# A fused decoder layer on one core: TensorE's semaphore waits moved ahead of the last two matmuls of the group in front

## The reference

```python
x = layernorm(x + self_attn(x))              # 128 sequences of 128 tokens, D = 256, 16 heads of 64, causal
x = layernorm(x + cross_attn(x, ctx, mask))  # 16 heads of 16, keys masked, biases
x = layernorm(x + ffn(x))                    # two groups of 32 experts, hidden 128, top 2 of each, SwiGLU
```

## Time and profile before

| | |
|---|---|
| median of 3 runs | 4513.68 us (4513.43 to 4518.73) |
| the profiled execution | 4515.24 us, span 4513.5 us |
| TensorE busy over the span | 4395.4 us (97%), 38848 matmuls |
| VectorE, ScalarE, GpSimd busy | 3689.1 (82%), 3288.8 (73%), 2752.3 us (61%) |
| TensorE busy, 300 to 3,200 us | 2897.93 us |
| granted TensorE clock | 0.99 over the span |

### The profile page before, as it was taken

How to read it: one execution, slowest core, us unless ns; L and a number is a source line. 1 busy time by engine, 2 the same in 40 slices (tenths; PEclk the granted TensorE clock), 3 DMA queues, 4 the chain that set the end, 5 groups by cost and what they waited for, 6 DMA issues and landing times. The chain is left out here.

```text
span 4513.5 us, 129797 instructions
## 1 busy us (share of the span) xinstructions
PE 4395.4 (97%) x38848; PEld 3808.0 (84%) x38848; DVE 3689.1 (82%) x18057; ACT 3288.8 (73%) x12741; POOL 2752.3 (61%) x3747
## 2 busy tenths in 40 slices
PE   7999999999999999999999999999995899999998
PEld 6888888888888888888888888888884778878876
DVE  4788888888888888888888888888886466658888
ACT  5888888888888888888888888888884444444443
POOL 3466666666666566666665666666656455557777
PEclk9999999999999999999999999999997999999999
DMA  5121221111221211112211111112115599988998
GB/s 169 47 71 65 68 68 62 65 66 64 68 67 66 67 65 65 66 64 67 69 66 66 67 65 65 65 64 71 65 60 166 177 356 343 315 284 285 309 307 287
DMA packets 477421, 552.08 MB, mean 122 GB/s; under 512 B 55632, under 2 KB 408144, under 8 KB 476240
## 3 DMA queue, kind: packets, MB, share of 16 engines
q1 hardware_dynamic: 350800, 296.21, 20.5%
q0 software_dynamic: 52224, 146.87, 8.6%
q10 hardware_dynamic: 73728, 100.70, 7.3%
HBM read 266.21 MB, written 277.35 MB: 120 GB/s over the span
## 5 line engine op out<-in xcount | busy, mean ns | idle before, releaser
L898 ACT ACTIVATE prob<-prob,negmax 128x128 f32<-128x128 f32 x2048 | 796.5, 391 | 298.0 <-DVE negmax L1032 298.0
L898 ACT ACTIVATE xprob<-xprob,xnegmax 128x128 f32<-128x128 f32 x2048 | 797.8, 396 | 4.3 <-DVE xnegmax L1032 4.3
L1364 POOL DMA_INDIRECT y_d<-y,to x576 | 563.9, 979 | 352.2 <-DVE y L1506 325.8
L1032 DVE CUSTOM_DVE_ANT_0 prob<-bank,causal 128x128 f32<-128x128 f32 x2048 | 453.1, 285 | 303.2 <-PE bank L787 277.8
L634 POOL DMA_INDIRECT xs_d<-xrow,place x512 | 561.8, 1097 | 134.0 <-issue 133.0
L1417 PE MATMUL bank<-moe,xgT 128*128 x2304 | 595.4, 381 | 0.9 <-issue 0.6
L597 POOL TENSOR_TENSOR rs<-spread_v,minus_half 128x1 f32<-128x1 f32 x256 | 146.8, 573 | 644.1 <-DVE spread_v L1106 643.9
L1080 DVE TENSOR_TENSOR xprob<-xprob,xinv 128x512 f32<-128x512 f32 x512 | 482.9, 943 | 17.5
L580 POOL CAST yTh<-yT 128x512 fp32r<-128x512 f32 x256 | 206.0, 805 | 441.1 <-ACT yT L934 441.1
L685 PE MATMUL bank<-xT0h,wqkv 128*128 128x256 f32 x2048 | 437.4, 298 | 20.4 <-DVE wqkv L434 11.3
L1032 DVE CUSTOM_DVE_ANT_0 xprob<-bank,xmask 128x128 f32<-128x128 f32 x2048 | 451.6, 286 | 0.3 <-PE bank L787 0.3
(11 more groups left out here) (174 smaller groups left out, 13327.6 us busy)
## 6 DMA issues: line engine op xcount, KB each, us to landing
xg<-xs_d SPq DMA_DIRECT2D x576, 129.0 KB
xs_d<-blank SPq DMA_DIRECT2D x248, 272.0 KB
rows<-y_d ACTq DMA_DIRECT2D x256, 256.0 KB
xT_s<-xT SPq DMA_DIRECT2D x128, 128.0 KB, 2.5
cT<-cT SPq DMA_DIRECT2D x128, 128.0 KB, 2.1
x_s<-x SPq DMA_DIRECT2D x128, 128.0 KB
x_d<-x SPq DMA_DIRECT2D x128, 128.0 KB, 1.9
sums<-x_d ACTq DMA_DIRECT2D x128, 128.0 KB
```

What stands on the lines that cost most here:

```text
L898: last = nc.scalar.activation(dst[:, h, :], dst[:, h, :], ACT.Exp, bias=src_bias[:, h:h + 1], scale=-1.0, accum_out=acc[:, h:h + 1])
L1032: last = nc.vector.tensor_tensor_reduce(dst[:, h, :], heads(h), bias[:, :], -1.0, float("inf"), ALU.add, ALU.min, least[:, h:h + 1])
L1364: nc.gpsimd.indirect_dma_start(y_d[:, :], bass.IndirectOffsetOnAxis(ap=to[:, m % NTO:m % NTO + 1].bitcast(U32), axis=0), y_s[q][:, :], Non ...
```

## The change

Each group is cut in two functions: one with its waits (`..._needs`) and one with its matmuls, which takes as argument `ahead` a function that makes the waits of the group behind it. It is called ahead of the last two matmuls (of `x1t`, `x2t`, `o2`, `xv` and `route`, which have only two, ahead of all). Where a group isn't live in a step, `ahead` is called in its place. Two waits stay at the head of their group: that of `xq` (behind `v1`), and that of `rank` (behind `xk`). `score` of the next step is waited for inside `cross_mix`. The waits are the same semaphores and values, the matmuls the same in the same order.

```diff
-                    def chunks(out_ap, lhs, rhs, n=KC):
+                    def chunks(out_ap, lhs, rhs, n, ahead):
                         for k in range(n):
+                            if k == max(n - 2, 0):
+                                ahead()
                             last = nc.tensor.matmul(out_ap, lhs(k), rhs(k), start=(k == 0), stop=(k == n - 1))
                         return last
 
-                    def split_chunks(out_ap, lhs, rhs, n):
+                    def split_chunks(out_ap, lhs, rhs, n, ahead):
 
                         todo = [(k, *hs) for k in range(n) for hs in PASSES]
                         for i, (k, a, b) in enumerate(todo):
+                            if i == len(todo) - 2:
+                                ahead()
...
-                    def turn(n, side):
+                    def turn_needs(n, side):
 
                         if not live(n - 1):
                             return
...
+                    def turn(n, side, ahead):
+
+                        if not live(n - 1):
+                            ahead()
+                            return
                         for i in range(PH):
+                            if i == PH - 2:
+                                ahead()
                             last = nc.tensor.transpose(SCORES[side][:, i * P:(i + 1) * P], prob[:, (n - 1) % 2, side * PH + i, :], ident[:, :])
                         last.then_inc(turned, 1)
...
+                        first = "qk2" if n % 2 else "qk0"
+                        score(n, lambda: cross_score_needs(n))
+                        cross_score(n, lambda: job_needs(n, first))
                         if n % 2 == 0:
...
+                            job(n, "qk0", lambda: job_needs(n, "o2"))
+                            job(n, "o2", lambda: job_needs(n, "qk1"))
+                            job(n, "qk1", lambda: turn_needs(n, 0))
+                            turn(n, 0, lambda: turn_needs(n, 1))
+                            turn(n, 1, lambda: cross_turn_needs(n, 0))
+                            cross_turn(n, 0, lambda: job_needs(n, "x1t"))
+                            job(n, "x1t", lambda: cross_turn_needs(n, 1))
+                            cross_turn(n, 1, lambda: job_needs(n, "v1"))
+                            job(n, "v1", nothing)
+                            job_needs(n, "xq")
+                            job(n, "xq", lambda: job_needs(n, "xv"))
+                            job(n, "xv", lambda: mix_needs(n))
                         else:
...
+                            job(n, "qk2", lambda: job_needs(n, "x2t"))
+                            job(n, "x2t", lambda: job_needs(n, "o1"))
+                            job(n, "o1", lambda: turn_needs(n, 0))
+                            turn(n, 0, lambda: turn_needs(n, 1))
+                            turn(n, 1, lambda: job_needs(n, "route"))
+                            job(n, "route", lambda: job_needs(n, "qk3"))
+                            job(n, "qk3", lambda: cross_turn_needs(n, 0))
+                            cross_turn(n, 0, lambda: cross_turn_needs(n, 1))
+                            cross_turn(n, 1, lambda: job_needs(n, "xk"))
+                            job(n, "xk", nothing)
+                            job_needs(n, "rank")
+                            job(n, "rank", lambda: job_needs(n, "v0"))
+                            job(n, "v0", lambda: mix_needs(n))
+                        mix(n, lambda: cross_mix_needs(n))
+                        cross_mix(n, lambda: score_needs(n + 1) if n < TO else None)
```

More of the change, by code:

```diff
@@ L698, in job @@
                         free_bank(n, name)
+                        if name in QK:
+                            if b < 2:
+                                pe.wait_ge(*LOW_DONE[is_key(b)])
+                            pe.wait_ge(x_split, b // 2 + 1)
+                        elif name in ("v0", "v1"):
+                            if b == 0:
+                                pe.wait_ge(*LOW_DONE[2])
+                        elif name == "o1":
+                            if b == 0:
+                                pe.wait_ge(*LOW_DONE[3])
+                            pe.wait_ge(y_split, 2 * b + 2)
+                        elif name == "o2":
+                            pe.wait_ge(xyT_in, 2 * b + 2)
+                        elif name == "x1t":
+                            pe.wait_ge(x1_ready, b + 1)
+                        elif name == "x2t":
+                            pe.wait_ge(x2_ready, b + 1)
+                        elif name == "xq":
+                            pe.wait_ge(moved["x1t"], b + 1)
+                        elif name == "xk":
+                            pe.wait_ge(cT_in[b % 2], (b // 2 + 1) * 16)
+                        elif name == "route":
+                            pe.wait_ge(moved["x2t"], b + 1)
+                        elif name == "rank":
+                            pe.wait_ge(hot_ready, b + 1)
+                    def job(n, name, ahead):
+                        b = job_of(n, name)
+                        if b is None:
+                            ahead()
+                            return
                         o, p = jb(n, name), b % 2
@@ L764, in masked_out, with score_needs @@
                         wait(pe, xmaxed, min(2 * (n - CROSS) + cross_side + 1, ALL))
-                    def score(n):
+                    def score_needs(n):
+                        if not live(n):
+                            return
                         b, g = heads_of(n)
@@ L771, in score @@
                         banks_empty(n)
+                    def score(n, ahead):
+                        if not live(n):
+                            ahead()
+                            return
+                        b, g = heads_of(n)
                         for pair in range(PH):
+                            if pair == PH - 1:
+                                ahead()
                             for side in (0, 1):
@@ L776, in score, with cross_score_needs @@
                         last.then_inc(scores, 1)
-                    def cross_score(x):
+                    def cross_score_needs(n):
+                        x = n - CROSS
+                        if not live(x):
+                            return
                         b, c = heads_of(x)
@@ L783, in cross_score @@
                             pe.wait_ge(xk_ready, b + 1)
-                        banks_empty(x + CROSS)
+                        if not live(n):
+                            banks_empty(n)
+                    def cross_score(n, ahead):
+                        x = n - CROSS
+                        if not live(x):
+                            ahead()
+                            return
+                        b, c = heads_of(x)
                         for r in range(4):
+                            if r == 2:
+                                ahead()
                             rows = slice(r * ROWS, (r + 1) * ROWS)
@@ L813, in cross_turn, with mix_needs @@
                             wait(pe, xprobT_in, 2 * (x - 2) + side + 1)
+                    def cross_turn(n, side, ahead):
+                        x = n - CROSS
+                        if not live(x - 1):
+                            ahead()
+                            return
                         for i in range(PH):
+                            if i == PH - 2:
+                                ahead()
                             last = nc.tensor.transpose(SCORES[2 + side][:, i * P:(i + 1) * P], xprob[:, (x - 1) % 2, side * PH + i, :], ident[:, :])
                         last.then_inc(xturned, 1)
-                    def mix(n):
+                    def mix_needs(n):
                         if not live(n - 1):
@@ L826, in mix @@
                             pe.wait_ge(moved["v1"], b + 1)
+                    def mix(n, ahead):
+                        if not live(n - 1):
+                            ahead()
+                            return
+                        b, g = heads_of(n - 1)
                         for pair in range(PH):
+                            if pair == PH - 1:
+                                ahead()
                             for side in (0, 1):
@@ L850, in double_step @@
                     def double_step(n):
+                        if n == FROM:
+                            score_needs(n)
                         if n == 0:
```

85 lines of the change are left out of this document (27 added, 58 removed).

## The result

The changed kernel takes 4525.61 us (median of 13 runs, 4521.9 to 4533.73), the kernel before 4514.05 us (13 runs, 4510.57 to 4522.0). The ratio is 1.0025, with a 95% interval of 1.0017 to 1.0034: 11.6 us slower. The profiled execution has a span of 4532.0 us.

A forecast was written before the change was run, and what follows sets the result against it. TensorE was taken to bound the kernel, standing still where `route` waits for VectorE's late x2T copy. 13.5 us (that wait) + 1.5 us (first and last steps) = 15.0 us on 4513.68 gave 4529 us; range 4519 to 4540 us.

The forecast's parts named there:

- Part 1: TensorE's group heads: asking earlier for waits already met gains zero; upper bound 7 us, at steps from 256-column products to transposes.
- Part 2: `route`'s wait, moved ahead of two transposes of `turn(n, 1)`, delays `route` 0.218 us in 62 late steps: 13.5 us.
- Part 3: ScalarE's copies to probT after `turn` slip some 0.2 us, absorbed before the move of v; costs nothing, otherwise 12 us more.
- Part 4: `cross_turn(n, 1)` in even steps and `turn` in normal odd steps keep margins (0.16 us in the latter); costs nothing, otherwise 13 us.
- Part 5: First and last steps: some seven stalls each also delay the two instructions behind the moved wait; 1.5 us, bounds 0 and 3.

The follow-up runs named there:

- e7: The changed kernel with the waits of `route` and `qk3` both put back at the heads of their groups; 1.0007 of the kernel before.
- e6: The kernel before with two more long-met waits ahead of every TensorE group from step 1 on; 1.0017 of the kernel before.
- e2: The kernel before with only `route`'s wait moved, ahead of the last two transposes of `turn(n, 1)`; 4525.73 us, ratio 1.0026.
- e3: The kernel before with only `route`'s wait moved, ahead of all four transposes of `turn(n, 1)`; 4545.74 us, ratio 1.0066.
- e5: The changed kernel with VectorE's copy of x2T ahead of `cross_normalise` in odd steps; 0.9985 of the kernel before.
- e1: The changed kernel with `route`'s wait alone put back at the head of its group; 4524.82 us, ratio 1.0026.
- e10: The kernel before with the two waits of `qk3` made a second time, ahead of `route` and behind its own waits; ratio 1.002.
- e8: The kernel before with four more long-met waits for `route`, written behind its wait for x2T; 0.9994 of the kernel before.
- e4: The kernel before with VectorE's copy of x2T ahead of `cross_normalise` in odd steps; ratio 0.9986.

## Why the prediction was right, point by point

- **What bounds it.** Right. TensorE sets the time, and apart from the gaps at changes of tile the place where it stood still in the window was the late release of `route`, 57 times.
- **Part 1, waits already met.** Right. e7 leaves all the other moves in and is at 1.0007 (0.6 us in the 230 steps); the distance from `score` to `cross_score` is 1.09 to 1.10 us after as before; the gaps in front of `mix` and `cross_mix` are unchanged. The 7 us that I granted the 0.13 to 0.12 us as an upper bound were not there either: the step to the transposes is still 0.13 us (1526.81 to 1526.94). The rule of the Trainium skill (50 to 100 ns for a sequencer's read of a semaphore, "Advanced Engine Details and Errata", Network/Comms) isn't contradicted as a duration, 51 ns stand in the trace; but e6 shows that this reading is hidden, 31 groups in two steps, except where TensorE already waits or the release has only just come.
- **Part 2, the wait of route.** Right in mechanism, place and count; the term was mis-sized. I took 2 x 0.109 = 0.218 us a late step, it measured 0.17. The two transposes don't run at their steady distance: the first load starts after a stall, and the second follows it after 0.20 - 0.14 = 0.06 us, then `route` after 0.11. 0.17 x 57 in the window, and about as much for each of the 5 outside it, gives 10.5 us instead of 13.5. The steps agree: the late ones go from 14.34 to 14.51 us, and the 230 steps lose 10.65 us. e2 shows that this one wait is the change (1.0026 against 1.0025), e3 that it grows with the work behind the release, e5 that it vanishes with the late release.
- **Part 3, ScalarE's slip.** Right: 0.21 us for the pair of copies, 0.2 expected, and its waits for TensorE before the copies of v (99.4 us in all before, 99.6 after) are as they were.
- **Part 4, the next nearest waits.** Right: L859 stands idle in 57 steps, not in twice as many. The margin of the normal odd step, 0.16 us, held.
- **Part 5, filling and draining.** 1.5 us, not separable: 11.6 us measured less 10.5 is 1.1, within the interval of 8 to 15 us.
- **The sum.** 15.0 us forecast, 11.6 measured; 4529 against 4525.61. Of the 3.4 us between them 3.0 are the 0.05 us a late step of part 2. The mechanism was right; this one term was too large.
- What the prediction did not see: that the change makes another wait dear. `qk3`'s waits were moved ahead of both matmuls of `route`, that is right behind a wait that blocks. In the changed kernel this is covered, because the two transposes stand between them (the gap behind the release is filled by them); in e1, where they don't, it costs 0.23 - 0.11 = 0.12 us a late step, 7 us in all. That is the lower end of e1's interval (7 to 16 us), but its trace agrees: 7.0 us in the 230 steps. The 4 us by which e1's median lies above lie outside these steps, if they are anything. e10, with the same 0.11 us, is at 9 us (3 to 16) and at 6.2 us in the 230 steps.

"Perfetto Trace Analysis", section on the Tensor Engine Instruction, of the Trainium skill says that the sequencer pushes an instruction into a wait queue and can then fetch the next. The trace agrees where the wait is met: the eight transposes of `turn` run from one side to the other at the common 0.109 us, with a wait between them. Behind a blocked wait e1, e7 and e10 show a cost, 0.11 us for a further wait instruction.

## What to carry to other kernels

Moving a wait up in an engine's queue cost nothing here while it was met (e7), and hid nothing, since the engine had work in front of it anyway; where it wasn't met, it held back everything that it was moved past (e2, e3). So before moving waits, measure for each the distance from the producer's end to the place where it is asked for now and then; move only those with room, and put work of the engine between a late producer and its consumer rather than behind the wait. The gain was on the other side: make the late producer earlier, and look at once for the release that is the next late one, since here 10 of 16 us stood behind it.

## What the runs showed of the hardware that I had not expected

- Behind a wait that blocks, a further wait instruction on TensorE, though met, delays the next weight load by 0.11 us (0.11 us after VectorE's end in e7, 0.23 in e1, 0.22 in e10). Met waits that run ahead of the blocking one cost nothing (e8).
- How the waits of one load are packed goes with the latency of the release: 0.07 us from VectorE's end to the load when the blocking semaphore is in the last wait instruction together with another (e8), 0.11 us in an instruction of its own (the kernel before, e7). At `rank` it is 0.05 us where the load itself carries the wait (e4) and 0.22 us where the added waits have pushed it into an instruction of its own with another one behind (e6).
- Behind a stall, the load of the second transpose follows the first after 0.06 us instead of 0.11 us (the changed kernel; in e3 the four loads take 0.42 us instead of 0.46).
